# A state-space mixer's pair loop: additions, copies and chunk sums moved between DVE, POOL, ACT and PE

## What is computed

```python
dt = softplus(dt_raw + dt_bias)                 # (B, T, 64 heads)
a = exp(-exp(A_log) * dt)                       # decay of a step
phi = cumsum(dt, axis=1)[..., None] * rope_freqs
Bh = rope(rms(Braw) + B_bias, phi)              # (B, T, 64, 64)
Ch = rope(rms(Craw) + C_bias, phi)
u = xh * dt[..., None]                          # (B, T, 64, 8)
def step(h, inp):
    a_t, u_t, b_t, c_t = inp
    h = a_t[..., None, None] * h + u_t[..., None] * b_t[:, :, None, :]
    return h, einsum('bhpn,bhn->bhp', h, c_t)
y = 64 ** -0.5 * ys + D_param[None, None, :, None] * xh
```

## Time and profile before

| | |
|---|---|
| median of 3 runs | 1896.92 us (1890.16 to 1899.69) |
| profiled execution, its own time | 1888.91 us |
| its span | 1887.1 us |
| mean granted PE clock | 0.84 |

### The profile page before, as it was taken

The page is one execution under the profiler, slowest core; times in us unless marked ns, Lnnn a source line. Parts: engine busy times, 40 slices in busy tenths (PEclk is TensorE's granted clock), DMA queues, the critical chain, the costliest instruction groups (busy, mean ns, idle before and its releaser), DMA issues.

```text
span 1887.1 us, 40832 instructions
## 1 busy us (share of the span) xinstructions
PE 1415.2 (75%) x15288; PEld 824.9 (44%) x15368; DVE 1147.9 (61%) x2261; ACT 836.9 (44%) x1360; POOL 429.5 (23%) x326
## 2 busy tenths in 40 slices
PE   0368898595578898898636788859567888988882
PEld 0253332243256665666424433214243556656662
DVE  7456781413677777776455578441455777777736
ACT  0272456332355555553317245644134555555440
POOL 7220000040033343443012000002302333333400
PEclk9677999797688888888867699989777888888896
DMA  4200000100422111120010000010014211111100
GB/s 160 96 1 2 2 2 1 45 1 12 92 46 47 44 44 44 44 48 20 1 46 1 2 2 2 2 45 1 12 30 97 46 45 44 44 44 44 35 1 23
DMA packets 36685, 62.44 MB, mean 33 GB/s; under 512 B 15040, under 2 KB 24000, under 8 KB 35792
## 3 DMA queue, kind: packets, MB, share of 16 engines
q1 hardware_dynamic: 36272, 58.70, 12.6%
q10 hardware_dynamic: 288, 2.10, 0.3%
HBM read 20.79 MB, written 6.23 MB: 14 GB/s over the span
## 4 chain that ended last, share of the span: by engine, by line
issue 63%; PE 14%; POOL 9%; DVE 8%; POOLq 3%; DVEq 1%; ACT 1%; DMA 0%; SPq 0%; ACTq 0%
POOL region L643 4%; POOL region L642 3%; PE PS L1537 3%; PE PS L1522 2%; POOLq L631 2%; PE PS L1570 1%; POOL region L635 1%; POOL region L623 1%; PE PS L1576 1%; PE PS L1509 1%; DVE region L1180 1%; PE PS L1553 1%; DVE S L1175 1%; DVE region L1144 1%; DVE region L1145 1%
## 5 line engine op out<-in xcount | busy, mean ns | idle before, releaser
L642 POOL TENSOR_TENSOR region<-region 128x1024 f32<-128x1024 f32 x64 | 150.7, 2355 | 614.7 <-DVE region L1146 614.7
L1017 DVE TENSOR_REDUCE region<-PS 128x1 f32<-128x512 f32 (+3 forms) x304 | 180.5, 652 | 79.8 <-PE PS L1340 43.6
L723 ACT ACTIVATE region<-PS 128x512 f32<-128x512 f32 x288 | 164.1, 597 | 123.1 <-PE PS L1387 80.6
L1537 PEld LDWEIGHTS PS<-region 64*64 64x64 f32 x4096 | 143.3, 140 | 48.4 <-issue 48.4
L1143 DVE SCALAR_TENSOR_TENSOR region<-region,rows 128x1024 f32<-128x1024 f32 x64 | 82.2, 1284 | 132.4 <-POOL region L643 103.5
L1537 PE MATMUL PS<-region 64*64 64x64 f32 x4096 | 160.8, 229 | 0.9 <-issue 0.7
L1276 PE MATMUL PS<-ident,S 128*128 128x128 f32 x128 | 35.0, 429 | 168.2 <-DVE S L914 165.1
L819 ACT COPY region<-PS 128x512 f32<-128x512 f32 x128 | 74.8, 584 | 192.1 <-PE PS L1522 192.1
L630 POOL TENSOR_TENSOR region<-region 128x512 f32<-128x512 f32 x28 | 35.5, 1268 | 544.3 <-ACT region L765 543.5
L643 POOL TENSOR_TENSOR region<-region 128x1024 f32<-128x1024 f32 x64 | 151.2, 2362 | 0.0
L1337 PE MATMUL PS<-region 96*128 96x512 bf16 (+3 forms) x384 | 115.2, 350 | 24.8 <-DVE region L1017 16.5
(11 more groups left out here) (252 smaller groups left out, 2984.0 us busy)
## 6 DMA issues: line engine op xcount, KB each, us to landing
region<-region SPq DMA_DIRECT2D x256, 128.0 KB, 2.3
region<-parts_scratch SPq DMA_DIRECT2D x8, 448.0 KB, 9.0
region<-in_L_ffn_factors_dram SPq DMA_DIRECT2D x2, 1024.0 KB, 7.1
X<-in_L_attn_x_dram SPq DMA_DIRECT2D x2, 1024.0 KB, 5.8
region<-w1T_scratch SPq DMA_DIRECT2D x2, 1024.0 KB, 4.8
region<-w2T_scratch SPq DMA_DIRECT2D x2, 1024.0 KB, 6.9
out_dram<-X SPq DMA_DIRECT2D x2, 1024.0 KB, 5.0
parts_scratch<-region SPq DMA_DIRECT2D x2, 768.0 KB, 3.2
```

What stands on the lines that cost most here:

```text
L642: nc.gpsimd.tensor_tensor(PB1[:, r], PB1[:, r], PB2, ALU.add).then_inc(s_bb, 1)
L723: nc.scalar.activation(PB[:, u % (2 * G0), :], PS[:, 2 + u % 2, :], ACT.Exp).then_inc(s_p, 1)
L1017: nc.vector.reduce_max(MB[:, h:h + nh, k0 // 4], src, AX).then_inc(s_smu, 1)
L1537: last = mm(PS[q, 2 + half, (i % 4) * P + 64 * c:(i % 4) * P + 64 * c + 64], PB1[q, r, t], PC1[q, r, t], start=True, stop=True, tile_posit ...
```

## The change

Four things are moved.

1. The addition for C goes from POOL to DVE (`rotated_c`, behind `mixing`); POOL adds B only.
2. `chunk_sums` stands ahead of `phases` in PE's slot.
3. `inputs` goes from DVE to ACT, at the end of odd slots, as copies: no factor is left in UI, and US is copied from a new tile XW, made once in a block. The multiplication by D goes into `pair_outputs` on DVE.
4. For that the step sizes are folded into the decay arguments: ACT takes the logarithm of dt/8 (LN), DVE subtracts it from the log decay (LS), POOL splits LS in three bf16 parts (LQ), and SP stores those and loads NL from them. WH uses LS too, so that WT holds the whole factor and XW = x times WT.

```diff
@@ sync
-                    if lo == 0:
-                        for a in range(3):
-                            sp.dma_start(NL[64 + 16 * a:80 + 16 * a], parts_d[HEADS:, a].rearrange("h (k s) -> k h s", s=Q)
-                                         ).then_inc(s_nl, 16)
+                sp.wait_ge(s_lq, b + 1)
+                sp.dma_start(sources_d, LQ[64:128]).then_inc(s_lqs, 16)
+                sp.wait_ge(s_lqs, (b + 1) * 16)
+                for a in range(3):
+                    sp.dma_start(NL[64 + 16 * a:80 + 16 * a], sources_d[:, a].rearrange("h (k s) -> k h s", s=Q)
+                                 ).then_inc(s_nl, 16)
@@ gpsimd
+                pool.wait_ge(s_lh, b + 1)
+                nc.gpsimd.tensor_tensor(LQ[64:128, 0], LS[64:128], onesc[64:128].to_broadcast([HEADS, T]), ALU.mult)
+                pool.drain()
+                nc.gpsimd.tensor_tensor(LS[64:128], LS[64:128], LQ[64:128, 0], ALU.subtract)
+                pool.drain()
+                nc.gpsimd.tensor_copy(LQ[64:128, 1], LS[64:128])
+                pool.drain()
+                nc.gpsimd.tensor_tensor(LQ[64:128, 2], LS[64:128], LQ[64:128, 1], ALU.subtract).then_inc(s_lq, 1)
...
-                        nc.gpsimd.tensor_tensor(PC1[:, r], PC1[:, r], PC2, ALU.add).then_inc(s_bc, 1)
@@ scalar
+                act.wait_ge(s_cum, b + 1)
+                nc.scalar.activation(LN[64:128], PS[64:128, 4:6, :].rearrange("p k t -> p (k t)"), ACT.Ln,
+                                     scale=float(NS) ** -0.5).then_inc(s_ln, 1)
...
+                def inputs(n, k):
+                    act.wait_ge(s_zc, at(b, n, 3))
+                    act.wait_ge(s_yt, at(b, n, 3))
...
+                    for c in range(2):
+                        for h in range(2):
+                            q, t = slice(64 * c, 64 * c + 64), slice(64 * h, 64 * h + 64)
+                            nc.scalar.copy(UI[t, 2 * m:2 * m + 2, c, h].rearrange("p r d t -> p t r d"), x[q, :, :, h])
...
+                        last = nc.scalar.copy(US[q, m, :, :, :, :, c].rearrange("p t r h d -> p t (r h) d"), w[q])
+                    last.then_inc(s_u, 2)
@@ vector
-                nc.vector.tensor_scalar(DT8, DT[:, :, 0], float(NS) ** -0.5, None, ALU.mult)
...
+                dve.wait_ge(s_ln, b + 1)
+                nc.vector.tensor_tensor(LS[64:128], LH[64:128], LN[64:128], ALU.subtract)
...
-                nc.vector.tensor_tensor(DTW, DT8, WT, ALU.mult).then_inc(s_prep, 1)
+                nc.vector.tensor_tensor(XW.rearrange("p t (h d) -> p (t h) d", d=HD), XS.rearrange("p t (h d) -> p (t h) d", d=HD),
+                                        WT.rearrange("p t h -> p (t h)").unsqueeze(2).to_broadcast([P, NT * HEADS, HD]),
+                                        ALU.mult).then_inc(s_prep, 1)
...
-                def inputs(n, k):
...
+                def rotated_c(n, k):
+                    dve.wait_ge(s_pm, at(b, n))
+                    nc.vector.tensor_tensor(PC1[:, k % 2], PC1[:, k % 2], PC2, ALU.add).then_inc(s_bc, 1)
...
                     nc.vector.tensor_tensor(YT, y[:, 0], e, ALU.mult)
+                    nc.vector.tensor_tensor(own, own, d, ALU.mult)
...
                             mixing(n - 1, k + 3)
+                        rotated_c(n, k)
                         if k % 2 == 1 and not (first and k == 1):
                             pair_outputs(n - 3)
-                        if k % 2 == 1 and not (last and k == 3):
-                            inputs(n + 1, k + 1)
@@ tensor
+                        chunk_sums(n, k)
...
                             phases(it + 1, k - 1)
-                        chunk_sums(n, k)
```

More of the change, by code:

```diff
@@ L30 @@
 BLOCKS = 4
-ARENA = 41600
+ARENA = 43392
 C = 256
@@ L261, in build @@
         XV = arena.take(4, T)
-        DT8 = arena.take(NT, HEADS)
-        DTW = arena.take(NT, HEADS)
+        XW = arena.take(NT, DI)
         ELT = arena.take(NT, HEADS)
@@ L272, in build @@
         DTE = arena.take(NT, HEADS)
-        WT = arena.take(NT, HEADS)
+        WT = DTA
         BD = arena.take(NT, 4, P)
@@ L277, in build @@
         LH = arena.take(T)
-        LRES = arena.take(T)
+        LRES = BSQ.rearrange("p t n -> p (t n)")
         LP = arena.take(3, T, dt=BF16)
@@ L281, in build @@
         WH = arena.take(T)
-        LCH = arena.take(PAIRS, T // Q)
-        RST = arena.take(T)
+        LCH = DTE.rearrange("p t h -> p (t h)").rearrange("p (r k) -> p r k", r=PAIRS)
+        LQ = arena.take(3, T, dt=BF16)
+        RST = LQ.rearrange("p q t -> p (q t)").bitcast(F32)[:, 0:T]
+        LN, LS = WH, CUM
         prep_used = arena.used
@@ L847, in slots @@
                         turn_copy(n, k, 1)
+                        if k % 2 == 1 and not (last and k == 3):
+                            inputs(n + 1, k + 1)
                 for k in range(2):
                     sines(k, k)
+                act.wait_ge(s_prep, b + 1)
+                inputs(0, 0)
                 slots(0, True, False)
@@ L1192, in pair_outputs @@
                     dve.drain()
-                    own = XS[:, :, bass.ds(n * 16, 32)].rearrange("p t (e d) -> p t e d", d=HD)
                     nc.vector.tensor_tensor(own, own, YT, ALU.add).then_inc(s_yd, 2)
@@ L1201, in slots @@
                             mixing(n - 1, k + 3)
+                        rotated_c(n, k)
                         if k % 2 == 1 and not (first and k == 1):
                             pair_outputs(n - 3)
-                        if k % 2 == 1 and not (last and k == 3):
-                            inputs(n + 1, k + 1)
-                dve.drain()
-                inputs(0, 0)
                 slots(0, True, False)
```

46 lines of the change are left out of this document (21 added, 25 removed).

## The result

The kernel after takes **1842.96 us** (median of 4 runs, 1831.32 to 1858.52); the kernel before, on the same chip, 1894.46 (1890.16 to 1899.69). The ratio is 0.9736, 95% interval 0.9703 to 0.9769: faster by 2.6%, where 5.5% and 1793 us were forecast. The range ended at 1840, so the time lies outside it. The gain was half of the forecast, and the clock rival stood at 1864.

The account below looks back on a forecast made before the run. Chains of waits bound the kernel, no engine being full; afterwards PE sets the beat. 62 beats from 11.52 to 9.7 us give -113, preparations +9: -104 from 1896.9, so 1793 us, range 1765 to 1840.

Parts of the forecast that it names:

- The addition for C: DVE's even slot: starts at 7.25 when POOL's addition for B ends, takes 1.23, ends at 8.5 us.
- the clock rival: Pair loop: some PE wait stays in every second slot, clock does not recover; beat 10.85, 1864 us; chance 12%.
- PE's slot at full clock: Pair loop on PE: 9.33 us of matmul, 0.3 waiting for ACT's copy, 0.05 for odd gaps: 9.7 us.
- what put it down to 1.2 was the wait for the scan, and that goes: PE's clock in the pair loop: expected at 2.4 GHz throughout, with PE 96% busy; beat 9.7 us.
- ACT's copies: Six input copies in every second slot: 2.5 us, 1.2 a pair; ACT at 7.5 to 8.5 of 9.7, no cost.
- The table rival: Pair loop on ACT: table switches behind the new copies cost twice 1.3 us more, ACT needs 10.6; 1849 us; chance 3%.
- The slow rival: Pair loop on ACT: the inputs' scattered writes make copies slow; at 2 us each beat 12.8, 1985 us; chance 4%.
- the one in which the gain cancels: Pair loop on POOL: B's addition takes as long as both did; beat about 11.5, within 0.5% of 1900; chance 3%.
- the preparation: Work ahead of each block's pair loop: delay +4.4 us a block, 1.4 to 6.8; +9 for both.
- its own sign of being wrong: Ahead of each block's pair loop: the prediction is wrong if the preparation costs more than 7 us a block.
- The chain up to the negation: Preparation: log decay ready about 489.2, POOL's four operations done at 501, negation of FZ 10.55 us, ending at 511.5.
- XW ... is held behind the negation: Preparation on DVE: the XW product, 4.48 us, waits until 511.5 and ends at 516.

Follow-up runs that it names:

- e17: Kernel after with the rounding matmuls of the phases over 64 rows instead of one: 1812.37 us, ratio to before 0.9565.
- e5: Kernel after with the rounding matmuls of the phases over 96 rows instead of one, added weight rows zero: 1792.6 us, ratio to before 0.9477.
- e9: Kernel after with e5's tiles of 96 partitions and fills, but the rounding matmuls using one row: 1838.06 us, ratio to before 0.9713.
- e14: e5 with the six copies of the inputs back on DVE: 1839.96 us, ratio to before 0.9706.
- e1: Kernel after with the negation of FZ on POOL put back ahead of its wait for the log decays: 1830.35 us, ratio to before 0.9665.
- e16: e12 with POOL's four operations of the split done as four on DVE: 1783.6 us, ratio to before 0.9415.
- e12: e5 with the negation of FZ first and SP's store and first load of the sources earlier: 1788.56 us, ratio to before 0.9441.
- e6: Kernel after without the four rounding matmuls of each pair, a part of the computation left out: 1795.07 us, ratio to before 0.9483.

## Why the prediction was wrong, step by step

- **In the loop the engine that sets the beat was right.** With the chunk sums first and the inputs away, DVE's chain no longer holds PE, and PE sets the beat. PE's slot at full clock was forecast at 9.7 and measures 9.69 in both windows above, and 9.74 over the whole loop of e17. DVE was forecast at 9.5 and measures 9.50 to 9.54 in e5, where it is the bound. The chunk sums wait 0.26 for ACT's copy, as the earlier trace rows had it, in about half of the pairs (3.7 us in all over 26 slots).
- **The step that failed first:** "what put it down to 1.2 was the wait for the scan, and that goes". The clock's fall in slot 4 came behind a wait, and I made the wait its cause. After, PE has next to no waits and the clock still falls, in slots busy for 98 to 100%. The phases hold one-row matmuls; with 64 rows in them the clock stays full (e17), with 96 unused it does not (e9), and with 96 in use and PE idle for 11% of the loop it is full too (e14; 0.98 in block 1). Price: 10.24 - 9.74 = 0.5 us a beat, 31 us over 62 beats, of the 33 that the loop's forecast missed. (The Trainium skill, "TensorE: Matmul & The Clock Gate", section "Part 1: The HAM clock gate", says that the gate goes by how busy PE has been; by busy time alone the trace disagrees, 98% at 0.93 in after and 89% at 1.00 in e14.) In the kernel before, 96 rows raised the clock from 0.85 to 0.90, no further. That the waits hold down the rest there is likely and not shown.
- **The clock rival** had the right place and the wrong cause. It put the beat at 10.85 by a wait in every second slot; the clock came back for four slots in eight, and no wait was needed to lose it.
- **The addition for C** starts at the scan's end, 0.7 us before I had it, and takes 1.76 on average instead of 1.23. The one at 611.62 takes 1.86 and starts while POOL's addition for B (610.05 to 612.40) still runs. It ends 8.4 us behind the products' start, forecast 8.5. The step from an even slot is then 8.74 in e5.
- **ACT's copies** take 2.6 us for six, as taken from the 0.41 row. ACT is busy for 200 of 267 us, 7.7 a pair, and PE waits for it 5.3 us in all. The table rival is out: behind the copies above the next table load starts at 622.57 and its activation at 623.86, 1.29 later. The slow rival is out with the 2.6 us. So is the one in which the gain cancels: POOL's additions for B keep 2.35 us in the loop.
- **The second step that failed** is the preparation: +11.8 each in place of +4.4, beyond the 7 us that the prediction named as its own sign of being wrong. The chain up to the negation came as forecast: it ends at 514.69, 510.4 if the 4.3 us by which this preparation starts later are taken off, forecast 511.5. The step that failed is that XW starts at that end. "XW ... is held behind the negation" was right but counted too little: the 48 scalings of BD ahead of it (8.3 us together before, from 493.59 to 501.92; the expectation of e1 miscounts them as 24) were held as well, though each has one SBUF input. In DVE's timeline the first of them stands for 10.57 beside the negation from 503.38, where it takes 0.27 once POOL is idle; XW then starts at 522.70, 8.0 us behind the negation's end. PE waits 13.60 for the scalings, so the phases and the first Sin come as late. A slip of the sum is small beside this: 516 + 2.4 + 2.3 is 520.7 and not 520.9.

```profile
497.04 2.77 DVE L1154 TENSOR_TENSOR region<-region,spread 64x512 f32<-64x512 f32 x1
...
504.20 10.57 DVE L1166 TENSOR_SCALAR region<-region,rstd 128x128 f32<-128x128 f32 x1
...
514.88 0.27 DVE L1166 TENSOR_SCALAR region<-region,rstd 128x128 f32<-128x128 f32 x1
...
522.70 4.41 DVE L1175 TENSOR_TENSOR region<-region 128x4096 f32<-128x4096 f32 x1
532.71 1.28 DVE L1190 SCALAR_TENSOR_TENSOR region<-region,rows 128x1024 f32<-128x1024 f32 x1 [5.61 <-DMA region<-region]
```

  POOL's split had already stretched DVE's operations before that: L1154 takes 2.77 and, in e16, with POOL idle, 1.01. (The Trainium skill, "SBUF — State Buffer", section "Who interferes with whom", of which the prediction used the part on two SBUF inputs, describes the shared ports as an exclusive lock, and says that a `tensor_scalar` too can take them, in the modes that use two ports. The scalings are such operations. In which mode they ran no run shows, but the trace agrees that POOL's negation stopped one with a single SBUF input.)
- **What the rest of the preparation is.** Of 11.8 the negation is worth 3.2 to 3.8 (e1), the split on POOL another 1.8 to 3.1 (e12 to e16), both from the profiles. e16 still has 52.4 and 50.9 against 46.6 of before. Of these 4.3 to 5.8, SP's rows put 5.1 ahead of the store of LP, in both blocks, on DVE, which there makes LS and its four operations of the split first. From that store to the first products e16 takes 23.4 and 22.0, before 22.9 and 22.8, though the sources' store and load now run in the same queue. This is read from rows; no run took the operations or the transfers away. Nor is it shown what makes up the rest of e1's median beyond its two preparations.

## What to carry to other kernels

When a clock falls behind a wait, the wait is not yet its cause: look whether it falls in stretches without one, and at what those matmuls fill. Here four matmuls of a pair with one row of weights cost 31 us of clock and some 14 of steps, and with zero rows added to them (e5) the kernel was no slower than without them (e6). Work moved off an engine pays only when that engine sets the beat: the same three moves were worth nothing to 17 us at the lower clock and 12 to 47 at the full one, so find and remove the bound first, then judge the parts. A long operation on POOL that is moved onto the path stopped DVE's one-input scalings beside it here, so each instruction queued behind such an operation must be counted.

## What the hardware showed unexpectedly

- The granted clock of the loop against the rows of four matmuls in some 164 a pair: 0.93 with one row, 0.94 with 32, 1.00 with 64 and 96; the moving side has as many rows as the weights. What lies between 32 and 64 was not tried. Without the four matmuls (e6) it is 0.98 and 0.96.
- A change from weights of 96 rows to 1, 32 or 64 and back spaces the matmul starts by 0.31 to 0.33 us in place of 0.22.
- An 11.31 us operation on POOL stopped a 128x128 scaling on DVE, 0.27 us by itself, for 10.57.
